# Attention stage of a transformer layer: minima of key halves combined once for four query tiles, two vector operations as scalar-tensor-tensor, and the row-sum matmuls placed behind the value matmuls

## The reference

```python
q, k, v = (split_heads(t) for t in (xn @ Wq, xn @ Wk, xn @ Wv))   # 16 heads of 64
q, k = (_rope(q), _rope(k))
sim = jnp.einsum('bhid,bhjd->bhij', q, k) * SCALE
attn = jax.nn.softmax(sim, axis=-1)
out = jnp.einsum('bhij,bhjd->bhid', attn, v)
return out.reshape(b, n, HEADS * DIM_HEAD) @ Wout + bout
```

## Time and profile before

| what | value |
|---|---|
| median of 3 runs | 2224.7 us (2223.3 to 2225.09) |
| profiled execution, its time | 2221.72 us |
| profiled execution, its span | 2219.8 us |
| PE busy | 1910.8 us, 86% |
| DVE busy | 1721.6 us, 78% |
| POOL busy | 1492.2 us, 67% |
| ACT busy | 813.5 us, 37% |

### The profile page before, as it was taken

The page is one execution under the profiler, slowest core; times in us unless marked ns, Lnnn a source line. Parts: engine busy times, 40 slices in busy tenths (PEclk is TensorE's granted clock), DMA queues, the critical chain, the costliest instruction groups (busy, mean ns, idle before and its releaser), DMA issues. The chain is left out here.

```text
span 2219.8 us, 30955 instructions
## 1 busy us (share of the span) xinstructions
PE 1910.8 (86%) x11492; PEld 1201.5 (54%) x11492; DVE 1721.6 (78%) x2251; ACT 813.5 (37%) x1012; POOL 1492.2 (67%) x691
## 2 busy tenths in 40 slices
PE   1377788658999999999999999999999999999779
PEld 0266678634555555555555555555555555555379
DVE  8799999748787778888787777888778777888144
ACT  1111112103444444444444444444444444444332
POOL 2355545316877887888887787888877778788700
PEclk8589989869999999999999999999999999999889
DMA  8000110130111120111112111111221111100175
GB/s 289 37 29 29 40 43 33 37 104 29 25 40 43 30 82 30 44 30 42 42 39 79 33 44 30 42 32 40 63 59 35 39 43 31 30 25 25 39 275 185
DMA packets 128057, 125.58 MB, mean 57 GB/s; under 512 B 40752, under 2 KB 92592, under 8 KB 127792
## 3 DMA queue, kind: packets, MB, share of 16 engines
q1 hardware_dynamic: 127920, 123.77, 17.9%
HBM read 83.36 MB, written 40.37 MB: 56 GB/s over the span
## 5 line engine op out<-in xcount | busy, mean ns | idle before, releaser
L1070 POOL TENSOR_TENSOR acc<-acc,prob 128x1024 f32<-128x1024 f32 x384 | 947.9, 2469 | 223.6 <-ACT prob L1113 198.2
L955 DVE TENSOR_REDUCE half_max<-m_ps 128x2 f32<-128x1024 f32 x512 | 623.5, 1218 | 322.3 <-PE m_ps L829 319.2
L1113 ACT ACTIVATE prob<-s_ps 128x1024 f32<-128x1024 f32 x512 | 500.1, 1025 | 425.3 <-PE s_ps L853 423.3
L868 PE MATMUL o_ps<-prob,v 128*64 128x512 f32 x2048 | 492.6, 602 | 0.0
L829 PE MATMUL m_ps<-k_hi,q_hi 64*128 64x512 f32 x1024 | 239.0, 463 | 61.8 <-DVE half_max L955 58.3
L868 PEld LDWEIGHTS o_ps<-prob,v 128*64 128x64 f32 x2048 | 130.0, 136 | 244.7 <-issue 179.2
L1052 POOL TENSOR_TENSOR turned<-straight,shuffled 128x512 f32<-128x512 f32 x128 | 179.1, 1399 | 95.2 <-DVE shuffled L987 95.2
L898 PE MATMUL misc_ps<-xT,wqk 128*128 128x512 f32 x768 | 219.8, 423 | 17.7 <-DMA xT<-xn_scratch 10.2
L898 PEld LDWEIGHTS misc_ps<-xT,wqk 128*128 128x128 f32 x768 | 139.0, 194 | 143.1 <-issue 108.2
L1070 POOL TENSOR_TENSOR acc<-prob 128x1024 f32<-128x1024 f32 x64 | 168.2, 2629 | 60.2 <-ACT prob L1113 60.2
L853 PE MATMUL s_ps<-max_rows,ones_r 64*128 64x512 f32 x1024 | 202.9, 393 | 0.0
(11 more groups left out here) (126 smaller groups left out, 2421.9 us busy)
## 6 DMA issues: line engine op xcount, KB each, us to landing
wqk<-wp_scratch SPq DMA_DIRECT2D x32, 512.0 KB, 4.4
inv_rows<-inv_scratch SPq DMA_DIRECT2D x128, 128.0 KB, 2.9
o_scratch<-o_norm SPq DMA_DIRECT2D x64, 256.0 KB, 2.0
o_in<-o_scratch SPq DMA_DIRECT2D x8, 2048.0 KB, 9.8
xn_scratch<-xnT SPq DMA_DIRECT2D x8, 1024.0 KB, 4.3
xT<-xn_scratch SPq DMA_DIRECT2D x8, 1024.0 KB, 6.6
wv<-wp_scratch SPq DMA_DIRECT2D x32, 256.0 KB, 3.5
wp_scratch<-wp_hl SPq DMA_DIRECT2D x8, 768.0 KB, 3.9
```

Source lines behind the costliest of these rows:

```text
L868: ins = nc.tensor.matmul(o_ps[head * DH:(head + 1) * DH, :], v[s // 2 % 2][:, kt, s % 2, at:at + DH], prob[n % SLOTS][:, head, :], start=k ...
L955: nc.vector.tensor_reduce(half_max[:, t % 2, part, :], m_ps[:, :, :], axis=AX.X, op=ALU.max, negate=True).then_inc(half_maxed, 1)
L1070: nc.gpsimd.tensor_tensor(acc[b][:, :, :], first, prob[n % SLOTS][:, :, :], ALU.add).then_inc(added, 1)
L1113: nc.scalar.activation(prob[n % SLOTS][:, :, :], s_ps[n % 2][:, :, :], ACT.Exp).then_inc(exp_done, 1)
```

## The change

Three edits, all in `attention_part`.

1. `half_max` gets room for four query tiles in each of two buffers, and `combine` is called once for each half step (rounds 3 and 7) on 2 x 4 numbers of each partition, in place of once in every round on 2. `turn_max` and `maximum` wait for the new counts of `max_done`.
2. `combine` and `normalise` are written as `scalar_tensor_tensor` (times 1.0, then the minimum or the product) in place of `tensor_tensor`.
3. TensorE issues `column_sums` behind the two `values` of its round in place of ahead of them.

```diff
-    half_max = sb("half_max", [P, 2, 2, 2], F32)
+    half_max = sb("half_max", [P, 2, 2, 2, GRP], F32)
...
             def turn_max(s, half):
                 begin("turn", s, half)
-                pe.wait_ge(max_done, s * QT + 4 * half + 4)
+                pe.wait_ge(max_done, 2 * s + half + 1)
...
                         guess(s + 1, 2 * r + 1)
+                    for n in (s * UNITS + 2 * r - 2, s * UNITS + 2 * r - 1):
+                        if 0 <= n < STEPS * UNITS:
+                            values(n)
                     if r == 2 and scoring(s - 1):
                         column_sums(s - 1, 1)
                     if r == 6 and scoring(s):
                         column_sums(s, 0)
-                    for n in (s * UNITS + 2 * r - 2, s * UNITS + 2 * r - 1):
-                        if 0 <= n < STEPS * UNITS:
-                            values(n)
                     if r == 0 and scoring(s):
                         turn_max(s, 1)
...
             def maximum(s, i):
                 dve.wait_ge(guessed, s * UNITS + i + 1)
-                t, part = divmod(s * UNITS + i, 2)
-                if t >= 2:
-
-                    dve.wait_ge(max_done, t - 1)
-                nc.vector.tensor_reduce(half_max[:, t % 2, part, :], m_ps[:, :, :], axis=AX.X, op=ALU.max,
+                t, part = divmod(i, 2)
+                half = 2 * s + t // GRP
+                if half >= 2:
+
+                    dve.wait_ge(max_done, half - 1)
+                nc.vector.tensor_reduce(half_max[:, half % 2, part, :, t % GRP], m_ps[:, :, :], axis=AX.X, op=ALU.max,
                                         negate=True).then_inc(half_maxed, 1)
...
-            def combine(s, t):
-
-                dve.wait_ge(half_maxed, s * UNITS + 2 * t + 2)
-                cols = max_cols[t // 4][:, :].rearrange("p (h n) -> p h n", h=2)[:, :, t % 4]
-                nc.vector.tensor_tensor(cols, half_max[:, t % 2, 0, :], half_max[:, t % 2, 1, :], ALU.min).then_inc(max_done, 1)
+            def combine(s, half):
+
+                dve.wait_ge(half_maxed, s * UNITS + (half + 1) * QT)
+                cols = max_cols[half][:, :].rearrange("p (h n) -> p h n", h=2)[:, :, 0:GRP]
+                nc.vector.scalar_tensor_tensor(out=cols, in0=half_max[:, half, 0, :, :], scalar=1.0, in1=half_max[:, half, 1, :, :],
+                                               op0=ALU.mult, op1=ALU.min).then_inc(max_done, 1)
...
-                nc.vector.tensor_tensor(o_norm[b][:, :], o_raw[b][:, :], inv_rows[b][:, :], ALU.mult).then_inc(normed, 1)
+                nc.vector.scalar_tensor_tensor(out=o_norm[b][:, :], in0=o_raw[b][:, :], scalar=1.0, in1=inv_rows[b][:, :],
+                                               op0=ALU.mult, op1=ALU.mult).then_inc(normed, 1)
...
                         maximum(s + 1, 2 * r + 1)
-                        combine(s + 1, r)
+                        if r in (3, 7):
+                            combine(s + 1, r // 4)
```

## The result

The changed kernel takes 2237.6 us (median of 4 runs, 2235.2 to 2239.42) against 2224.3 us (4 runs, 2223.3 to 2225.09): 13.3 us slower, ratio 1.0059 with a 95% interval of 1.0042 to 1.0077. The forecast was 2242 in a range of 2222 to 2262. The profiled execution of the changed kernel took 2237.73 us, 16.0 more than that of before.

What follows compares the result with a forecast made beforehand. PE was taken to bound the kernel, so only its waits or added work count. Vector edits 0, exposed copy 17.7: 2221.72 + 17.7 = 2239.4 us profiled, plus 3.0 for the median, so 2242, range 2222 to 2262.

Steps and rivals of the forecast that it cites:

- Edits 1 and 2 give nothing: DVE's combinations and normalisations: a scalar-tensor-tensor with two SBUF inputs waits for POOL like a tensor-tensor, so 0 us gained.
- The combinations of rounds 4 and 5 pass their wait on: DVE, rounds 4 and 5: the `low` behind takes over the removed combination's wait for POOL, ending at the same moment.
- my 0.2: DVE, rounds 3 and 7: assumed 0.2 us for a combination on eight numbers, 0.04 more at two places a step.
- the upper bound of 0.677: DVE, rounds 3 and 7: the combination on eight numbers takes at most 0.677 us, which would cost 30 us.
- The row sums lose the cover of the copy: PE, rounds 2 and 6: the projection waits for ACT's row-sum copy, 0.30 us later at 59 places, 17.7 us.
- The rounding up from 0.27 to 0.30: Rough score to projection, 3.82 us against 3.55: the 0.27 us delay was taken as 0.30 for hundredths at borders.
- One side remark: ACT's row-sum copy: it comes about 1.9 us later for ACT, which has only PE's next scores to wait for.
- The price of the free scalar-tensor-tensor: Normalisations: rival that the form does not wait for POOL; 60 us go, 17.7 come, 2182 us; chance 0.11.
- the two stalls go: PE's rough score: if the form did not wait for POOL, both stalls of a step would vanish, worth 60 us.
- the copy hides after all: Row sums in rounds 2 and 6: case within the no-change rival, under 0.075 us lost at each of 59 places; chance 0.10.
- a change too small to measure: Whole kernel: rival that no change is measured, 2221 to 2229 us, say 2226; chance 0.10.
- A shifted meeting of POOL and normalisation: Rounds 3 and 7: rival that normalisation meets a whole POOL addition more, 2275 to 2300 us; chance 0.05.

Runs made afterwards that it cites:

- e2: Kernel before with the grouped combine and the scalar_tensor_tensor forms only, row sums ahead of the values as before: 2221.44 us, ratio 0.9993.
- e5: Kernel before with the normalisation replaced by a same-size DVE maximum with one SBUF input, leaving out the product: 2172.77 us, ratio 0.9774.
- e1: Kernel before with only the row-sum matmuls moved behind the values, vector operations as they were: 2240.11 us, ratio 1.0076.
- e10: e7 with the grouped combine and the scalar_tensor_tensor forms on top, row sums ahead of the values: 2159.63 us, ratio 0.9718.
- e7: Kernel before with normalisations moved from rounds 3 and 7 to 2 and 6, reciprocals from 1 and 5 to 0 and 3: 2174.53 us, ratio 0.9780.
- e3: Changed kernel with ACT copying the row sums twice, first into a buffer nobody reads: 2266.15 us, ratio 1.0198 against the kernel before.

## Why the prediction was right, point by point

**Edits 1 and 2 give nothing.** Right. The decision rested on POOL being held up by a `low` in step -2 and not on the 64 undisturbed rows, and e2 and the rows of the profile after bear it out: the waits at the rough score are unchanged (45.0 us in 59), the normalisation keeps a median of 1.77 us as a scalar-tensor-tensor, and `low` waits up to 2.31 us once no combination stands ahead of it. By the Trainium skill, page "SBUF — State Buffer", section "Who interferes with whom", a DVE instruction with two SBUF inputs contends with a GpSimd instruction that reads SBUF, and one with at most one does not (outside DVE's two-port modes). The trace agrees: 2.28 us with two of them at 1255.86, and with one never more than 0.686 in e5 and 0.692 in the product of L983.

**The combinations of rounds 4 and 5 pass their wait on.** Right: 1.70 us of combination and 0.68 of `low` have become 2.28 us of `low` in round 5. The combination on eight numbers takes 0.166 us at the least, where two numbers took 0.161, so my 0.2 was near enough and the upper bound of 0.677 was not touched.

**The row sums lose the cover of the copy.** Right, with the size of the term a little off. The links added to 3.82 us and the profile has 3.81. The rounding up from 0.27 to 0.30, for hundredths at borders, was not needed: 59 times 0.26 is 15.3 us, against the 17.7 of the sum, and a step became 50.67 us, not 50.76. The profiled execution grew by 16.0, e1 by 17.1, the medians by 13.3. e2's small gain may account for part of the difference of the last two, but its interval does not show it. One side remark of the prediction was wrong and touched nothing: ACT's copy comes 1.2 us later behind its rough score, not 1.9 (1238.46 - 1235.30 = 3.16 against 1230.49 - 1228.54 = 1.95), as the prediction's own links give.

**The price of the free scalar-tensor-tensor.** It was put at 60 us. That case did not come, but its price can be read: e10 differs from e2 only in where the normalisations and reciprocals stand, and the ratio goes from 0.9993 to 0.9718, 61 us. That is a stand-in for the free form, not the free form itself. Without the grouped minima it would have been about 50, as e5 and e7 show; the step "the two stalls go" left out the combination of round 0, which takes its time from the stall in front of it.

**The rivals.** That the copy hides after all fell with e3, and a change too small to measure fell with the result, whose interval starts at 9.3 us. A shifted meeting of POOL and normalisation did not come: 1.08, 0.68 and 2.88 us stand in the same order as before. (Its sum had a slip: 29 times 1 to 2 us on top of 2242 is 2271 to 2300, not 2275 to 2300.) A shift of that kind came in e5 and e7, between POOL and the combination of round 0, once the stall in front had been removed.

What stays open is whether edits 1 and 2 alone gain a microsecond or two; eleven runs of e2 against 21 of the kernel before do not tell.

## What to carry to other kernels

A row that never shows a wait proves nothing if the instruction ahead of it has always done the waiting; look for one that starts in the middle of what it might wait for, or for what it holds up on the other side. Work between two dependent steps on one engine may be cover for another engine's part of the chain: before moving a step, write down which wait each neighbour hides, and try the middle. And a removal that is worth nothing while a larger stall stands ahead of it can be worth something once that stall is gone, so try it again then.

## What the runs showed of the hardware that I had not expected

That removing a stall of PE made a DVE instruction on two numbers take 2.00 us in place of 0.55, since it then met the beginning of a POOL addition instead of its last part (0.55 us is the same combination of round 0 in the trace of before). And that the links of a chain over three engines (matmul end to ACT 0.05 us, copy 0.60, ACT to PE 0.05), each read from another place of the trace, the last even from a stretch in which PE's granted clock was 0.50 of its full 2.4 GHz (472 to 475 us), came out in the changed kernel as 0.05, 0.60 and 0.05 again.
